# State space stage: eight scan units in the ring, GpSimd's products over two units, and sums three units later

## What is computed

```python
proj = hidden_states @ W_in.T
u, gate = jnp.split(proj, 2, axis=-1)
...                                   # causal convolution with 4 taps over time
u = jax.nn.silu(conv(u) + conv_b)
ssm_p = u @ Wx.T
dt, Bm, Cm = jnp.split(ssm_p, [R, R + N], axis=-1)
...                                   # an RMS norm on each of the three
delta = jax.nn.softplus(dt @ Wdt.T + dt_bias)

def step(state, xs):
    d_t, B_t, C_t, u_t = xs
    dA = jnp.exp(d_t[..., None] * A)
    state = dA * state + (d_t * u_t)[..., None] * B_t[:, None, :]
    y_t = jnp.einsum('bdn,bn->bd', state, C_t)
    return (state, y_t)
...
y = jnp.swapaxes(ys, 0, 1) + u * D_param
y = y * jax.nn.silu(gate)
return y @ W_out.T
```

## Time and profile before

| | us |
|---|---|
| median of 3 runs (lowest to highest) | 1969.73 (1966.2 to 1977.37) |
| the profiled execution, its time | 1971.7 |
| the profiled execution, its span | 1969.9 |
| first scan of the stage to its last | 852.4 to 1842.2 |

### The profile page before, as it was taken

How to read it: one execution, slowest core, us unless ns; L and a number is a source line. 1 busy time by engine, 2 the same in 40 slices (tenths; PEclk the granted TensorE clock), 3 DMA queues, 4 the chain that set the end, 5 groups by cost and what they waited for, 6 DMA issues and landing times. The chain is left out here.

```text
span 1969.9 us, 24262 instructions
## 1 busy us (share of the span) xinstructions
PE 1608.2 (82%) x8168; PEld 855.9 (43%) x8168; DVE 1381.4 (70%) x2292; ACT 1091.1 (55%) x2026; POOL 1009.7 (51%) x598
## 2 busy tenths in 40 slices
PE   6888999999779983888597796987978879735768
PEld 2522233222155442665174573655746547402532
DVE  3258888887084115059989888889888898999323
ACT  2333666667621114367767567576675766754127
POOL 0000000001044003449998888989889988999303
PEclk8866999999875995889597796987968879756769
DMA  5311000000094439243544444535344444453122
GB/s 223 152 52 55 3 3 3 3 3 3 12 312 180 130 128 325 81 107 87 122 103 103 107 93 107 125 85 123 92 108 116 98 103 103 108 117 86 38 91 86
DMA packets 152988, 195.78 MB, mean 99 GB/s; under 512 B 17907, under 2 KB 123139, under 8 KB 151198
## 3 DMA queue, kind: packets, MB, share of 16 engines
q1 hardware_dynamic: 143692, 167.19, 32.3%
q0 software_dynamic: 4608, 16.80, 2.3%
q10 hardware_dynamic: 4564, 10.24, 1.4%
HBM read 141.81 MB, written 52.37 MB: 99 GB/s over the span
## 5 line engine op out<-in xcount | busy, mean ns | idle before, releaser
L1808 DVE TENSOR_TENSOR_SCAN ssm_scan<-ssm_psum,ssm_state,ssm_scan 128x256 f32<-128x256 f32 x1024 | 677.6, 728 | 67.8 <-ACT ssm_psum L1695 66.1
L1431 POOL TENSOR_TENSOR ssm_scan<-ssm_scan,ssm_bc 128x1024 f32<-128x1024 f32 x256 | 553.3, 2176 | 52.9 <-DVE ssm_scan L1808 51.8
L1695 ACT ACTIVATE ssm_psum<-ssm_rep,ssm_a 128x256 f32<-128x256 f32 x1024 | 430.9, 468 | 117.4 <-DVE ssm_scan L1808 115.0
L1535 PE MATMUL ssm_psum<-ssm_scan,ssm_select 128*32 128x256 f32 x2048 | 202.3, 476 | 214.5 <-POOL ssm_scan L1431 214.1
L1411 POOL TENSOR_TENSOR ssm_scan<-ssm_rep,ssm_bc 128x1024 f32<-128x1024 f32 x128 | 301.1, 2353 | 63.3 <-PE ssm_psum L1535 51.6
L641 ACT ACTIVATE att_probs<-att_psum 128x1024 f32<-128x1024 f32 x256 | 248.4, 1021 | 106.0 <-PE att_psum L577 105.8
L678 DVE TENSOR_REDUCE att_rowmax<-att_psum 128x1 f32<-128x512 f32 x448 | 277.9, 682 | 39.6 <-PE att_psum L559 39.5
L1535 PEld LDWEIGHTS ssm_psum<-ssm_scan,ssm_select 128*32 128x32 f32 x2048 | 45.7, 119 | 329.4 <-POOL ssm_scan L1431 225.6
L530 POOL COPY att_v<-v_tokens 128x128 f32<-128x128 f32 x8 | 2.3, 291 | 329.5 <-ACT att_out L635 329.5
L559 PE MATMUL att_psum<-att_k,att_q 72*128 72x512 bf16 x448 | 159.8, 397 | 3.7 <-DVE att_rowmax L678 2.2
L1793 DVE TENSOR_TENSOR ssm_scan<-ssm_rep,ssm_psum 128x1024 f32<-128x1024 f32 x128 | 155.5, 1215 | 10.4 <-PE ssm_psum L1535 8.1
(11 more groups left out here) (232 smaller groups left out, 1905.3 us busy)
## 6 DMA issues: line engine op xcount, KB each, us to landing
ssm_rep<-drive_rows SPq DMA_DIRECT2D x256, 256.0 KB, 4.6
qkv_wmod<-in_wmod SPq DMA_DIRECT2D x8, 1536.0 KB, 12.0
late_weights<-in_we SPq DMA_DIRECT2D x8, 1024.0 KB, 14.8
ssm_bc<-bc_rows SPq DMA_DIRECT2D x32, 256.0 KB, 5.0
drive_rows<-ssm_delta SPq DMA_DIRECT2D x64, 128.0 KB
drive_rows<-ssm_du SPq DMA_DIRECT2D x64, 128.0 KB
sorted_rows<-moe_zeros SPq DMA_DIRECT2D x1, 5888.0 KB, 18.9
moe_sorted<-sorted_rows SPq DMA_DIRECT2D x23, 256.0 KB, 3.5
```

The source lines that it names most:

```text
L1431: nc.gpsimd.tensor_tensor(read[:, Q % RING], drive[:, Q % RING], bc[:, c % 2, 1, gr, :].unsqueeze(1).to_broadcast([P, J, SW]), ALU.mult).t ...
L1535: last = nc.tensor.matmul(ps_y[t % 2][32 * j:32 * j + 32, :], select[:], read[:, Q % RING, j, :], start=(gr == 0), stop=False)
L1695: nc.scalar.activation(ps_decay[n % HALF_BANKS][:, i], rep[:, s % 2, 0, j, :], ACT.Exp, scale=amat[:, t, gr, j:j + 1]).then_inc(decay_done, 1)
L1808: nc.vector.tensor_tensor_scan(drive[:, Q % RING, j, :], ps_decay[(2 * Q + j // 2) % HALF_BANKS][:, j % 2], drive[:, Q % RING, j, :], stat ...
```

## The change

- The ring has eight slots (`RING = 8`).
- GpSimd's program works in pairs of units. Its `spread(s)` makes the drive products of both even units of tile `s` in one instruction of 2 x 4 x 256 elements, and it is called once a tile, in unit `gr == 1` of the tile before, ahead of that unit's C product. The C product is made in the odd units, for two units in one instruction. `drive_input` stays where it was: in `gr == 1`, behind the C product.
- TensorE sums unit `Q - 3` where it summed `Q` (`LAG = 3`), behind the misc of `q`.
- `gate_y` writes into `gate` in place (the buffer `y` is gone), one unit later (`GATE_Y = 3`). So the gate's projection of the next chunk is issued after the output projection of the chunk before: the two change places in `AT`, with their copies on ScalarE, and the SiLU of the gate goes from unit 20 to unit 31.
- In SyncE's queue the residual is loaded and the output stored elsewhere in the chunk.

```diff
-    RING = 4
+    RING = 8
...
-        y = sb("ssm_y", [P, 2, DT, SW])
...
-              9: ("conv", 3), 10: ("gate", 0), 11: ("gate", 1), 12: ("gate", 2), 13: ("rows", 0), 14: ("gate", 3), 15: ("square", 0),
-              16: ("out", 0), 17: ("out", 1), 19: ("rms", 0), 21: ("step", 0), 22: ("step", 1),
-              24: ("step", 2), 25: ("step", 3), 27: ("out", 2), 28: ("out", 3)}
+              9: ("conv", 3), 10: ("out", 0), 11: ("out", 1), 12: ("out", 2), 13: ("rows", 0), 14: ("out", 3), 15: ("square", 0),
+              16: ("gate", 0), 17: ("gate", 1), 19: ("rms", 0), 21: ("step", 0), 22: ("step", 1),
+              24: ("step", 2), 25: ("step", 3), 27: ("gate", 2), 28: ("gate", 3)}
...
-        U_COPY, CONV_OUT, GATE_OUT = {3: 0, 4: 1, 7: 2, 9: 3}, {6: 0, 8: 1, 10: 2, 12: 3}, {13: 0, 14: 1, 15: 2, 17: 3}
-        SILU, ROWS_OUT, RMS, GATE_SILU, H_OUT = 13, 16, 18, 20, 24
+        U_COPY, CONV_OUT, GATE_OUT = {3: 0, 4: 1, 7: 2, 9: 3}, {6: 0, 8: 1, 10: 2, 12: 3}, {18: 0, 19: 1, 29: 2, 30: 3}
+        SILU, ROWS_OUT, RMS, GATE_SILU, H_OUT = 13, 16, 18, 31, 24
...
-        OUT_COPY = {19: 0, 20: 1, 30: 2, 31: 3}
-        GATE_Y, DRIVE = 2, 1
+        OUT_COPY = {12: 0, 13: 1, 14: 2, 16: 3}
+        GATE_Y, DRIVE, LAG = 3, 1, 3
...
-                    if t == 1 and c >= 2:
-                        store(c - 2)
+                    if t == 5 and c >= 1:
+                        store(c - 1)
...
-                    if t == 2 and c >= 1:
+                    if t == 1 and c >= 1:
                         load_residual(c - 1)
...
-            def spread(Q):
+            def spread(s):
...
+                c, Q = s // DT, s * GROUPS
                 pool.wait_ge(rep_in[s % 2], 64 * (s // 2 + 1))
                 pool.wait_ge(bc_in[c % 2], 64 * (c // 2 + 1))
                 if Q >= RING:
-                    pool.wait_ge(sum_done, Q - RING + 1)
-                    pool.wait_ge(carry_done, (Q - RING) // 2 + 1)
-                nc.gpsimd.tensor_tensor(drive[:, Q % RING], rep[:, s % 2, 1],
-                                        bc[:, c % 2, 0, gr, :].unsqueeze(1).to_broadcast([P, J, SW]), ALU.mult).then_inc(pool_input, 1)
+                    pool.wait_ge(sum_done, Q + 2 - RING + 1)
+                    pool.wait_ge(carry_done, (Q + 2 - RING) // 2 + 1)
+                nc.gpsimd.tensor_tensor(drive[:, Q % RING:Q % RING + 3:2], rep[:, s % 2, 1].unsqueeze(1).to_broadcast([P, 2, J, SW]),
+                                        bc[:, c % 2, 0, 0::2, :].unsqueeze(2).to_broadcast([P, 2, J, SW]), ALU.mult).then_inc(pool_input, 2)
...
             drive_input(0, 0)
             drive_input(0, 1)
-            for Q in range(2):
-                if not ON_DVE[Q]:
-                    spread(Q)
+            spread(0)
             for c in range(SCH):
                 for q in range(UNITS):
                     t, gr = q // GROUPS, q % GROUPS
                     Q = c * UNITS + q
-                    if Q + 2 < SCH * UNITS and not ON_DVE[(q + 2) % UNITS]:
-                        spread(Q + 2)
-                    pool.wait_ge(scan_done, (Q + 1) * J)
-                    nc.gpsimd.tensor_tensor(read[:, Q % RING], drive[:, Q % RING],
-                                            bc[:, c % 2, 1, gr, :].unsqueeze(1).to_broadcast([P, J, SW]), ALU.mult).then_inc(read_done, 1)
+                    if gr % 2:
+                        if gr == 1 and c * DT + t + 1 < SCH * DT:
+                            spread(c * DT + t + 1)
+                        pool.wait_ge(scan_done, (Q + 1) * J)
+                        pair = slice((Q - 1) % RING, Q % RING + 1)
+                        nc.gpsimd.tensor_tensor(read[:, pair], drive[:, pair],
+                                                bc[:, c % 2, 1, gr - 1:gr + 1, :].unsqueeze(2).to_broadcast([P, 2, J, SW]), ALU.mult).then_inc(read_done, 2)
                     c2, t2 = ahead(c, t)
                     if c2 < SCH and gr == DRIVE:
                         drive_input(c2, t2)
...
                     for key in at(c, q):
                         misc(*key)
-                    sum_states(c, q)
+                    Q = c * UNITS + q - LAG
+                    if Q >= 0:
+                        sum_states(Q // UNITS, Q % UNITS)
+            for q in range(UNITS - LAG, UNITS):
+                sum_states(SCH - 1, q)
...
-                if c >= 2:
-                    dve.wait_ge(out_mm, (c - 1) * KT)
-                nc.vector.tensor_tensor(y[:, c % 2, t, :], ps_y[t % 2], gate[:, c % 2, t, :], ALU.mult).then_inc(ygate_done, 1)
+                nc.vector.tensor_tensor(gate[:, c % 2, t, :], ps_y[t % 2], gate[:, c % 2, t, :], ALU.mult).then_inc(ygate_done, 1)
```

More of the change, by code:

```diff
@@ L1377, in _ @@
             load_residual(SCH - 1)
-            store(SCH - 2)
             store(SCH - 1)
@@ L1399, in drive_input @@
                 nc.gpsimd.tensor_tensor(du[:, s % 2], delta[:, t, :], u[:, c % 2, t, :], ALU.mult).then_inc(du_done, 1)
-            def spread(Q):
-                c, q = Q // UNITS, Q % UNITS
-                t, gr = q // GROUPS, q % GROUPS
-                s = c * DT + t
+            def spread(s):
+                c, Q = s // DT, s * GROUPS
                 pool.wait_ge(rep_in[s % 2], 64 * (s // 2 + 1))
@@ L1520, in output @@
                 for t in range(DT):
-                    nc.tensor.matmul(bank("out", c, m)[:, 0:SW], wout[:, t, m * P:(m + 1) * P], y[:, c % 2, t, :], start=(t == 0), stop=False)
+                    nc.tensor.matmul(bank("out", c, m)[:, 0:SW], wout[:, t, m * P:(m + 1) * P], gate[:, c % 2, t, :], start=(t == 0), stop=False)
                 if m == 0:
@@ L1660, in copy_gate @@
                 if pair == 0 and c >= 2:
-                    act.wait_ge(ygate_done, (c - 1) * DT)
+                    act.wait_ge(out_mm, (c - 1) * KT)
                 nc.scalar.copy(gate[:, c % 2, 2 * pair:2 * pair + 2, :], halves("gate", c, pair)).then_inc(gate_out, 1)
```

## The result

The changed kernel takes **2242.5 us** (median of 4 runs, 2239.3 to 2255.1) against 1973.6 us for the kernel before on the same chip (the table ahead of the forecast has the median of three runs; this one has a fourth). The ratio is 1.137, with a 95% interval of 1.132 to 1.143: 13.7% slower. Forecast was 2219, in a range of 2135 to 2275.

A forecast was written before the change was run, and what follows sets the result against it. The changed kernel was taken as bound by GpSimd's one-tile loop through the DRAM round trip: 62 turns of 18.7 us plus 52 us of slow TensorE blocks, 248.9 us over the profiled 1971.7, less 2.0, gave 2219 us, range 2135 to 2275.

The forecast's parts named there:

- A closed loop with only one tile in it: 18.7 us a tile: GpSimd: drive products 4.55, C product 4.2, `du` 0.69, then the 9.3 us DRAM round trip before the next drive products.
- light turn: A tile's turn in GpSimd's loop without two big TensorE products in the way; claimed at 18.7 us.
- trip: Drive input stored to DRAM by SyncE and loaded back fourfold, from the end of `du` to the last landing: 9.3 us.
- the other turns: Turns of the stage outside the first and the heavy ones; forecast mean 18.8 us.
- 26 blocks, 52 us: TensorE's pairs of big products in tiles 0, 1, 3, 4, slowed by the lower clock: 2.0 us each over the loop.
- heavy turns: Turns of tiles 0, 1, 3 and 4 of chunks 1 to 6, with two big TensorE products; forecast mean 20.7 us.
- The blocks of chunk 0: Chunk 0 was to lack two blocks: its first tile doesn't wait, and no `out` comes before it.
- the rest of the edits: Gate SiLU at unit 31, `gate_y` at unit 3, moved residual load and store: claimed to lie under GpSimd's loop.
- No depth of the ring helps: Claim that more ring slots can't shorten GpSimd's 18.7 us loop, since no slot of the ring is in it.
- TensorE keeps its clock: Rival: the blocks on TensorE hide and only GpSimd's loop counts; 2167 us, chance 0.17.
- Loads in time: Rival: loads land in time and the loop of TensorE and GpSimd is the bound; about 2020 us, chance 0.06.
- VectorE as the bound: Rival: VectorE alone sets the pace and some 100 us of stalls go; 1870 us, chance 0.03.

The follow-up runs named there:

- the old order: Changed kernel with GpSimd's program of the kernel before (single instructions, their old order), all other edits kept: 1975.7 us, 1.000 against the kernel before.

## Why the prediction was right, point by point

- **"A closed loop with only one tile in it: 18.7 us a tile."** Right, and shown by moving its one movable part both ways. An undisturbed light turn is 18.75, with a trip of 9.44 for 9.3; 4.52 and 4.16 for the instructions (taken as 4.55 and 4.2), whose slopes from smaller shapes held. GpSimd's waits for the load come to 216 us with the row that names the scans (forecast: over 200), its busy time to 860.5 (about 870). The Trainium skill's 4.50 us for 2048 elements (GPSIMD Engine Reference, section 3.1) fits the drive product here (4.516) and is 8% too much for the C product (4.162); the 19 us that it would have added over the stage aren't in the trace.
- **Mean of the other turns.** The 36 turns that were to take 18.7 took 19.11 in the mean, 15 us more in all. 23 of them stand at 18.4 to 19.0, and 13 at 19.5 to 20.4. Of these 13, eight have the late issue of the store described above, in four the loads were issued 0.7 to 1.7 us late behind stores that were issued in time, and in one they landed late. The term "trip" was taken from one undisturbed trip, and I should have taken a mean over several.
- **"26 blocks, 52 us" at the lower clock.** The 24 heavy turns of chunks 1 to 6 exceed the loop by 1.85, not 2.0 (44 us against 48). The size was right. What makes it has two parts that overlap, since either one taken away frees most of it: the clock (filling the gaps gave 28 us back) and the joined product's late release (single products gave 33, with the first big product of 16 of the 24 blocks still slow), which stood in my sum only as 4.2 us of C product ahead of TensorE's sum. I had worked out that without slow blocks these turns hide under 18.7; the kernel with filled gaps bears that out at tiles 3 and 4.
- **The blocks of chunk 0.** The first tile indeed doesn't wait for TensorE. But the first of the 62 turns, tile 1 of chunk 0, was in the sum as one more block, 20.7 us, and took 30.7. GpSimd waits 16.73 us for TensorE in it, whose timeline has:

```profile
875.20 6.29 PE L1465 MATMUL ssm_psum<-ssm_h,late_weights 128*128 128x256 f32 x16 [0.56 <-ACT ssm_upre L1599]
...
889.58 0.64 PE L1531 MATMUL ssm_psum<-ssm_scan,ssm_select 128*32 128x256 f32 x8
...
902.30 0.64 PE L1531 MATMUL ssm_psum<-ssm_scan,ssm_select 128*32 128x256 f32 x8
```

The C product was done at 881.18, but the first sum starts at 889.58, since from 875.20 on TensorE works off products left over from preparing the first chunks, and more of them stand between the first sum and the last. This was the largest single miss, 10 us, in a term that I had counted as one block like any other. With the sums one unit late this turn took 19.6.
- In all the 62 turns took 1233.2 us against 1211 forecast, 22 more: 10 in the first turn, 15 in the 36 light ones, 1 in tile 4 of chunk 0 (21.3 for 20.7), and 4 less in the heavy ones. So the sum came near because each term was near, and hardly because errors cancelled. The profiled execution without its late start took 2240.0 against 1971.7 + 248.9 = 2220.6.
- **"Costs nothing": the rest of the edits.** Under the loop only the sums were tested, and there a lag of three instead of one costs 18 us. At the old order all of these edits can be read, and they come to nothing together (1.000). But they are not nothing each: late sums are worth 47 us there, and with them switched off the others cost as much. Which of the others (ring, gate and output products swapped, `gate_y` at unit 3) costs it was not separated; only that earlier gate products don't cure it. Nor is the stall gone that the change was to be free of: VectorE waits as long as before, elsewhere.
- **"No depth of the ring helps."** Argued from the loop, and not tried.
- **The rivals.** TensorE keeps its clock: no, the granted clock was 0.75, and the first big product was slow in all 24 heavy turns. Loads in time: no, but the kernels with `du` earlier are what that rival looks like when the load is taken out of the loop. It had been priced at 2020, without slow blocks; with joined products the kernel took 2082, and with single ones 2014. VectorE as the bound: VectorE idled for 391 of 1280 us.

## What to carry to other kernels

Take the instruction that starts a round trip and the one that waits for its landing, and count in program order what lies between them on their engine: if the sum is less than the trip and only one trip can be under way, the trip plus all the rest of the turn is the time of a turn. (That deeper buffers don't help then was argued here, not tried.) Joining two instructions saves little here (0.15 us of 4.3), and what waits for the first half comes about 2.2 us later, half the length, so join only where nobody waits for that half. A lag that takes a wait from one engine gives it to the consumer at the other end; try the steps between (here two units beat both none and three).

## What the runs showed of the hardware that I had not expected

- Issuing one and the same DMA from SyncE took 0.43 us as a rule and 1.17 to 1.86 us in 13 of the 62 turns, and the loads behind it were issued 0.7 to 1.9 us later than in the other turns; in a loop with one tile in it, that shows in the total.
- Between profiled executions the start of this stage varied from 844.2 to 868.3 us, more than most edits here are worth, with kernels of the same program ahead of it 9 us apart (849.2 and 858.1). Runs of one kernel spread by 15 us too (1969.3 to 1984.5 in ten). A gain must be read from medians, and beside them from the stage's own length.
- How long a gap was did not by itself decide at which clock TensorE went on. In the changed kernel sum and projection took 1.08 and 5.64 us after a gap of 4.55, and with the gap filled by idle matmuls 0.64 and 3.72. But in the kernel with single instructions the sum and the product of 16 matmuls behind it took 0.64 and 3.72 after a gap of 3.46, and 1.08 and 6.01 after one of 3.47. So a single turn that got faster proves nothing about the clock; count over all of them.
